# Block-sparse attention on one core: which transposed units ScalarE copies out of PSUM

## The reference

```python
xn = _layernorm(x, axis=-1)
x = x + _L1_attn_ref(xn, ...) + _L1_ffn_ref(xn, ...)

def _L1_attn_ref(x, w_qkv, b_qkv, w_out, b_out):   # 16 heads of 16 features, blocks of 128 rows
    bi = jnp.arange(L) // 128
    is_global = bi % 24 == 0                        # so block 0 only
    allowed = (bi[:, None] == bi[None, :]) | is_global[:, None] | is_global[None, :]
    qkv = x @ w_qkv.T + b_qkv
    scores = jnp.einsum('bhqd,bhkd->bhqk', q * scale, k) + where(allowed, 0, -inf)
    attn = jax.nn.softmax(scores, axis=-1)
    out = jnp.einsum('bhqk,bhkd->bhqd', attn, v)
    return out @ w_out.T + b_out
```

## Time and profile before

| | us |
|---|---|
| median of 3 timed runs | 3855.11 (3853.64 to 3855.38) |
| the profiled execution | 3852.84 |
| its span, first to last instruction | 3850.7 |
| a middle batch of the block-sparse stage | 73.8, some 75.2 |
| its last batch, from the result of the one before | 61.8 |

### The profile page before, as it was taken

The page is one execution under the profiler, slowest core; times in us unless marked ns, Lnnn a source line. Parts: engine busy times, 40 slices in busy tenths (PEclk is TensorE's granted clock), DMA queues, the critical chain, the costliest instruction groups (busy, mean ns, idle before and its releaser), DMA issues. The chain is left out here.

```text
span 3850.7 us, 48624 instructions
## 1 busy us (share of the span) xinstructions
PE 3230.5 (84%) x15980; PEld 1864.1 (48%) x15980; DVE 2634.9 (68%) x3666; ACT 1656.0 (43%) x4077; POOL 1587.6 (41%) x974
## 2 busy tenths in 40 slices
PE   2677787778787778599999959999999689999998
PEld 1224242424242434366666626666666355655665
DVE  6798989888888989477677725555555255555553
ACT  1554545454545454166555613333333133333332
POOL 1555554655455545200000035554455165555552
PEclk9889898988888888899999969999999899999999
DMA  1211111020202020100010020000000200000000
GB/s 47 99 44 61 47 58 72 32 93 11 93 11 93 11 88 11 41 29 26 22 33 27 12 75 12 21 16 16 16 16 11 68 17 22 22 22 22 22 16 17
DMA packets 82137, 141.89 MB, mean 37 GB/s; under 512 B 7730, under 2 KB 71302, under 8 KB 73878
## 3 DMA queue, kind: packets, MB, share of 16 engines
q1 hardware_dynamic: 73622, 132.66, 9.7%
q10 hardware_dynamic: 8448, 8.39, 0.7%
HBM read 119.54 MB, written 21.50 MB: 37 GB/s over the span
## 5 line engine op out<-in xcount | busy, mean ns | idle before, releaser
L902 PE MATMUL ps_y<-hb,ident 128*128 128x512 f32 x1024 | 588.0, 707 | 228.0 <-DVE hb L602 227.8
L492 POOL TENSOR_TENSOR hb<-bcB,du 128x1024 f32<-128x1024 f32 x256 | 604.3, 2374 | 374.0 <-PE ps_y L902 370.6
L592 DVE TENSOR_TENSOR_SCAN ps_dA<-ps_dA,hb 128x1024 f32<-128x1024 f32 x256 | 585.9, 2289 | 90.5 <-POOL hb L492 56.5
L902 PEld LDWEIGHTS ps_y<-hb,ident 128*128 128x128 f32 x1024 | 211.0, 221 | 510.3 <-DVE hb L602 305.3
L1691 POOL TENSOR_TENSOR c_pr<-c_pr,c_inv 128x512 f32<-128x512 f32 (+1 forms) x256 | 232.6, 934 | 411.6 <-DVE c_inv L1803 409.6
L2158 PE MATMUL c_ps_s<-c_hT,c_w 128*128 128x512 f32 x704 | 321.0, 603 | 17.2 <-DVE c_hid L1869 15.4
L1261 ACT ACTIVATE b_pr<-b_ps_s,b_negmax 128x256 f32<-128x256 f32 (+1 forms) x512 | 263.8, 527 | 164.8 <-DVE b_negmax L1175 162.9
L725 ACT ACTIVATE ps_dA<-delta,a_neg 128x511 f32<-128x511 f32 x512 | 329.4, 675 | 0.6
L1920 ACT ACTIVATE c_pr<-c_ps_s,c_negmax 128x256 f32<-128x256 f32 (+1 forms) x512 | 222.2, 446 | 246.5 <-DVE c_negmax L1798 246.5
L602 DVE TENSOR_TENSOR hb<-ps_dA,bcC 128x1024 f32<-128x1024 f32 x256 | 312.3, 1220 | 5.2
L1668 POOL TENSOR_TENSOR c_q_cos<-c_q_cos,c_q_sin 128x1024 f32<-128x1024 f32 x64 | 150.9, 2357 | 311.9 <-DVE c_q_sin L1777 311.9
(11 more groups left out here) (235 smaller groups left out, 6265.2 us busy)
## 6 DMA issues: line engine op xcount, KB each, us to landing
bcB<-bc_scratch SPq DMA_DIRECT2D x32, 1024.0 KB, 4.6
bcC<-bc_scratch SPq DMA_DIRECT2D x32, 1024.0 KB, 6.5
c_x<-stream_scratch SPq DMA_DIRECT2D x16, 512.0 KB, 5.0
c_xr<-stream_scratch SPq DMA_DIRECT2D x16, 512.0 KB, 4.4
xn<-in_x_dram SPq DMA_DIRECT2D x8, 512.0 KB, 7.2
xr<-in_x_dram SPq DMA_DIRECT2D x8, 512.0 KB, 4.0
x_scratch<-xr SPq DMA_DIRECT2D x8, 512.0 KB, 2.9
b_x<-x_scratch SPq DMA_DIRECT2D x8, 512.0 KB, 4.1
```

What stands on the lines that cost most here:

```text
L492: pool.tensor_tensor(hb[:, s % RING, :, :], bcB[:, states(g), :], bc(du[:, c % 2, :].unsqueeze(1), [P, NG, T]), ALU.mult)\
L592: dve.tensor_tensor_scan(flat(h_all), flat(h_all), flat(tile), 0.0, ALU.mult, ALU.add)\
L902: last = pe.matmul(ps_y[:, :], W["ident"][:, :], hb[:, r % RING, i, :], start=False, stop=(g == GROUPS - 1 and i == NG - 1))
```

## The change

ScalarE copied every fourth unit (u % 4 == 3): ten of 40, in every second step. Now it copies the odd units with one head: 1, 3, 5, 7, 21, 23, 25 and 27, eight of 40, one in each of the steps 2 to 5 and 12 to 15. VectorE copies the other 32, so both units of a pair wherever they have two heads. The counts of the two semaphores and the waits follow, and `weigh` waits once where all four of its units are VectorE's.

```diff
--- before.py
+++ after.py
@@ -935,6 +935,8 @@
     PAIRS = UNITS // 2
     QUADS = UNITS // 4
     HALF = QUADS // 2
+
+    BY_ACT = [u for u in range(UNITS) if u % 2 and len(UNIT[u][1]) == 1]
     TURN_LAG, PV_LAG = 2, 4
 
     AHEAD = 2
@@ -1010,8 +1012,8 @@
         max_ready = S("b_max", UNITS)
         exp_ready = S("b_exp", UNITS)
         p_turned = S("b_p_turned", UNITS)
-        pt_dve = S("b_pt_dve", 3 * QUADS)
-        pt_act = S("b_pt_act", QUADS)
+        pt_dve = S("b_pt_dve", UNITS - len(BY_ACT))
+        pt_act = S("b_pt_act", len(BY_ACT))
         pv_done = S("b_pv", QUADS)
         inv_ready = S("b_inv_ready", 1)
         inv_turned = S("b_inv_turned", 1)
@@ -1030,14 +1032,14 @@
             return len(KEYS[UNIT[u][0]])
 
         def copied_by_act(u):
-            return u % 4 == 3
+            return u in BY_ACT
 
         def wait_pt(eng, b, u):
 
             if copied_by_act(u):
-                eng.wait_ge(pt_act.s, pt_act.at(b, u // 4 + 1))
+                eng.wait_ge(pt_act.s, pt_act.at(b, BY_ACT.index(u) + 1))
             else:
-                eng.wait_ge(pt_dve.s, pt_dve.at(b, u // 4 * 3 + u % 4 + 1))
+                eng.wait_ge(pt_dve.s, pt_dve.at(b, sum(i not in BY_ACT for i in range(u + 1))))
 
         def key_blocks(rows, m, qt):
 
@@ -1266,8 +1268,8 @@
                 for s in range(AHEAD, PAIRS + TURN_LAG):
                     if s < PAIRS:
                         exponents(b, s)
-                    if (s - TURN_LAG) % 2:
-                        u = 2 * (s - TURN_LAG) + 1
+                    u = 2 * (s - TURN_LAG) + 1
+                    if copied_by_act(u):
                         act.wait_ge(p_turned.s, p_turned.at(b, u + 1))
                         if u >= 8:
                             act.wait_ge(pv_done.s, pv_done.at(b, u // 4 - 1))
@@ -1349,8 +1351,12 @@
 
             def weigh(b, w, more):
 
-                for u in (4 * w + 2, 4 * w + 3):
-                    wait_pt(pe, b, u)
+                if not copied_by_act(4 * w + 3):
+
+                    wait_pt(pe, b, 4 * w + 3)
+                else:
+                    wait_pt(pe, b, 4 * w + 2)
+                    wait_pt(pe, b, 4 * w + 3)
                 if w == 0:
                     pe.wait_ge(res_ready.s, res_ready.at(b, 0))
                 if w == HALF and more:
```

## The result

The changed kernel takes 3861.6 us (median of 17 runs, 3857.0 to 3871.8) against 3855.1 before (17 runs, 3851.9 to 3858.6). The ratio is 1.0021, with a 95% interval of 1.0013 to 1.0028. By the ratio it is slower by 0.21%, by the medians by 6.5 us or 0.17%; the forecast was 3860.0, from a sum of 4.8 us or 0.12% more.

What follows compares the result with a forecast made beforehand. Stalls of TensorE's queue were taken to bound the kernel. Seven batches at -0.08 + 0.83 - 0.27 = +0.48 (3.4 us) and the last at 1.4 gave +4.8 us on 3855.1: 3859.9, say 3860.0, range 3851 to 3867.

Steps and rivals of the forecast that it cites:

- The bound: Block-sparse stage: whether TensorE's queue stalls sets the pace, not VectorE's or ScalarE's busy time; TensorE busy 70.5 of 73.8 us.
- Units 1 and 21: Single-head copies moved to ScalarE: after unit 21's, the transposes of unit 23 start at 1746.87 instead of 1746.70, +0.17 us.
- Units 5 and 25: ScalarE copies behind two-head exponents: transposes of unit 27 +0.83 us late, those of unit 7 +0.24 in batches with statistics.
- Unit 11: At the normalisation, unit 13's transposes start at 1732.44 instead of 1732.85; the first half of a batch nets -0.08 us.
- Units 35 and 39: End of a batch, both copied by VectorE: the reciprocal's transposes start at 1768.42 instead of 1768.69, -0.27 us.
- The last batch: It has neither statistics nor normalisation, so both halves lose 0.83 us: 1.66 - 0.27 = 1.4 us.
- two places only: Before the change TensorE stalls on ScalarE's copies only ahead of the transposes of units 13 and 37, 0.84 us each.
- The dropped wait: In weigh, one semaphore poll fewer for two-head quads: taken as 0, at the other end a gain of 1.4 us.
- (B): ScalarE's copies of units 5 and 25 come before their readers, so only gains stay: -9.0 us, 3846.1; chance 0.08.
- (C): The 0.83 us is absorbed or the batch's end gains 0.57 to 0.65: sum 0 to +2 us, 3855 to 3857; chance 0.20.
- the 9.6 us: Weighed by the skill's advice, two more copies a batch on VectorE at 0.60 us cost up to 9.6 over eight batches.
- (A): TensorE's granted clock falls at bn_stats in all seven batches, four more at 1.4 us: +5.6 us, 3865.5; chance 0.20.

## Why the prediction was right, and where it was off

**The bound.** That stalls of TensorE's queue decide, and busy shares don't, held in each experiment: VectorE at 52.5, 53.6, 54.9, 56.0 and 57.1 us a batch goes with 75.2, 73.8, 74.3, 72.9 and 71.4, and 57.2 with 72.2.

Times in what follows count from the batch's mark, the start of the result of the batch before: 1713.65 in the rows of before, 1789.21 in the undisturbed batch above. What the first half of a batch gains (0.08) or both halves lose (0.75) is carried along.

**Units 1 and 21.** T(23) was put at 33.14 and stands at 33.13.

**Units 5 and 25.** T(7) was put at 9.80 and T(27) at 39.10; they stand at 9.81 and 39.09. Taking the two late copies away gave back 1.42 us a batch, where 0.24 + 0.83 were the net losses that the sum put there. The difference is not an error of the sum: without the late copy of unit 5 the place gains outright, because VectorE still has one copy less there. The prediction says that it is rid of units 1 and 3. Unit 3 was ScalarE's already; only unit 1 is new, and one copy is also what its times have (1717.89 for 1718.38).

**Unit 11.** T(13) was put at 18.79 and stands at 18.79. VectorE was next late, as said.

**Units 35 and 39.** T(37) was put at 52.10, T(39) at 53.62 and the transposes of the reciprocal at 55.52; they stand at 52.08, 53.61 and 55.58. The last is 0.06 late. They follow the reciprocal's end, 1844.66, by 0.13, not by the 0.06 that I had taken from copies. So the end gave 0.21 and not 0.27, and a batch +0.54 and not +0.48. The 0.13 isn't fixed to the reciprocal: in the last batch it is 0.05, as shown below. What makes the difference is open.

**The last batch.** This term was mis-sized: 1.4 forecast, 1.0 measured (62.88 - 61.88). I had taken the second half's loss for the first half too. But in the kernel before, T(5) waits there for ScalarE's copy of unit 3: it starts 0.12 behind that copy's end, 2166.83. In this batch T(2) to T(4) too start 0.12 behind the copies ahead of them, where it is 0.05 in the others. In the other batches the trace itself puts the 0.35 ahead of T(5) down to this copy, a third place beside the prediction's "two places only". Last batch, before: T(5), the scores of step 5, the first weighting:

```profile
2166.95 0.42 PEld L1346 LDWEIGHTS b_ps_t<-ident,b_pr 128*128 128x128 f32 x4 [0.35 <-issue]
2167.54 0.73 PEld L1332 LDWEIGHTS b_ps_s<-b_kf,b_qm 32*128 32x128 f32 x8 [0.17 <-issue]
...
2169.62 0.48 PEld L1367 LDWEIGHTS b_ps_o<-b_pt,b_v 128*32 128x32 f32 x19 [0.17 <-issue]
```

The same scores and weighting after:

```profile
2170.49 0.73 PEld L1334 LDWEIGHTS b_ps_s<-b_kf,b_qm 32*128 32x128 f32 x8 [0.17 <-issue]
...
2173.42 0.68 PEld L1373 LDWEIGHTS b_ps_o<-b_pt,b_v 128*32 128x32 f32 x25 [0.17 <-issue]
```

From the batch's mark (2160.65 and 2163.92) the scores come at 6.89 before and 6.57 after, 0.32 earlier, and the weighting at 8.97 and 9.50. The first half loses 0.53, not 0.83: VectorE, without the copy of unit 1, reaches the next maxima 0.5 earlier, and so unit 3's copy ends 0.49 earlier too (5.70 behind the mark, not 6.19). The prediction counted VectorE's head start in the other seven batches only. The second half loses 0.83 as forecast. The end gains 0.36, not 0.27. The reciprocal and its transposes, before and after:

```profile
2211.52 0.54 DVE L1204 RECIPROCAL b_inv<-b_den 128x64 f32<-128x64 f32 x1
2212.72 0.32 PEld L1402 LDWEIGHTS b_ps_t<-ident,b_inv 128*16 128x16 f32 x4 [0.20 <-issue]
```

```profile
2216.40 0.54 DVE L1206 RECIPROCAL b_inv<-b_den 128x64 f32<-128x64 f32 x1
2216.99 0.32 PEld L1408 LDWEIGHTS b_ps_t<-ident,b_inv 128*16 128x16 f32 x4 [0.50 <-DVE b_inv L1206]
```

They start 52.07 and 53.07 behind the mark, and 0.53 + 0.83 - 0.36 is the 1.0.

**The sum.** Seven times 0.54 and 1.0 make 4.8, the total of the forecast, by two errors that cancel; that part of the agreement is luck. The first batch isn't quite one of the seven, either: from the projections ahead of it (1636.18 and 1635.15) to its result it takes 77.46 us before and 78.18 after, 0.72 more and not 0.54, because T(6) waits 1.41 there in both and comes only 0.31 earlier, not 0.49. With it the schedule explains 5.0 us. In the profiles the seven bodies from the first result to the last (six middle, one last) take 513.5 us against 508.9. The span grew by 4.2.

**The dropped wait.** 0 was taken and 0 measured.

**The rivals.** (B), that ScalarE isn't late, is out: its copy of unit 25 starts at 1827.64, 1.81 us behind the start of the four exponents ahead of it, and T(27) waits 0.79 for it. (C), that gains and losses cancel, is out: a batch at full clock loses 0.54. So are the 9.6 us by which the prediction weighed two copies more on VectorE. The Trainium skill (Perfetto Trace Analysis, Optimizing Scalar/DVE Operations) advises handing work to ScalarE where VectorE is saturated. VectorE wasn't (54.9 of 74.3 us busy), and the three kernels with 34 and 36 copies a batch on it were faster than both. (A), the clock, is half borne out. The prediction put the idle time ahead of T(6) at 0.91; it is 1.23, since T(5) comes earlier as well. Both profiles of the kernel before and both of the changed kernel had three falls in six middle batches, so in the first pair of profiles it adds only 3 x 0.12 us (a fall costs 1.56 us now, 1.44 before). But the kernel with unit 5 late and unit 25 not had six of six.

**What stays open.** The medians differ by 6.5 and 7.0 us, and the schedule explains 4.8 to 5.0. By the intervals, 5.0 to 10.8 us and 3.5 to 11.2, that is at the lower edge of the first and inside the second. Part of the spread isn't of this stage: the result of its first batch stands between 1710.6 and 1723.8 us in twelve profiles whose code up to there is the same, save for that batch, while everything behind its last result takes 1625.6 to 1628.7. Falls of the clock come in the first batch too, ahead of that result: in four of the twelve profiles, among them the second one of the changed kernel. In the kernel with two waits in `weigh` the clock stood at 0.50 for some 10 us there. Whether the rest is more or longer falls in the timed runs, which leave no trace, isn't shown.

## What to carry to other kernels

When a copy moves from one engine to another, look at what stands ahead of it in the new engine's program order at that step, not at how busy the engine is: here a lag of two steps put the single-head copies behind two-head exponents. Write the recurrence for one batch out of the timeline's start times; it gave each place to 0.1 us, and worked through for other lists, with the statistics moved, it found a version 20 us faster, some 4 of them by falls of the clock that no longer came. Do it for the first and the last batch too, since their stalls are others.

## What the runs showed of the hardware

TensorE's granted clock fell to its 1.2 GHz level at the statistics in some batches and not in others of the same execution, with the same instructions and the same idle time ahead. Counted over six middle batches a trace: where unit 5 came late, ahead of T(7), 3, 3, 2, 6 and 1 of six (15 of 30); where it didn't and the statistics stood in step 3, 3 and 3 in the kernel before and none in four other kernels (6 of 36); with the statistics moved, none of 6. So more idle time there goes with more falls, but the kernel before and the one without units 11, 35 and 39 have the same T(6) wait of 1.4 us and half of the batches against none. The Trainium skill (TensorE: Matmul & The Clock Gate, Part 1) ties the clock to how busy the engine has lately been; the counts agree in direction. These are middle batches; the kernel without units 11, 35 and 39 had a fall in the stage's first batch. What picks the batch wasn't settled.

A fall isn't always 1.4 us. In the kernel with units 5 and 25 added, one batch ran over 13 us at 0.50 of the clock and took 79.8 us, 4.7 more than its neighbours, and two of its eight runs took 3880 us, 15 over the others. Whether those two had more of such stretches, no trace shows. In the last batch, where ten of the twelve profiles had a fall behind the transposes of the reciprocal, the part from these to the result took 9.8 us (9.5 once), and 8.1 in the two profiles without one.
